# A two-stage routed feed-forward and attention kernel: scatters issued at set points, and the weight preparation in another order

## The chip, the cores and the metric

One Trainium2 chip, one of its cores. The metric is the device time of one execution in microseconds (us). A core has five engines that run their own instruction streams and meet at semaphores: PE (TensorE, matrix products and transposes into PSUM), DVE (VectorE), ACT (ScalarE), POOL (GpSimd) and SP (SyncE, here the issuer of most DMAs).

## The reference

`_layernorm` is a plain layer norm; the outer three lines are the whole computation. x is [2, 2048, 256], that is 32 tiles of 128 tokens.

```python
def ffn(h):                                  # E = 4 experts, D = 256, H = 512
    g = softmax(layer_norm(h, rn_g, rn_b) @ router_w.T)
    top2_w, top2_idx = top_k(g, 2); top2_w /= sum(top2_w) + 1e-8
    hid = relu(layer_norm(einsum('bsd,edh->bseh', h, w1), ln_g, ln_b))
    out = sum over the top 2 of top2_w * einsum('bseh,ehd->bsed', hid, w2)
    return layer_norm(out, on_g, on_b)
def attn(x):                                 # 16 heads of 16, causal, no softmax
    Q, K, V = heads(x @ Wq.T + bq), heads(x @ Wk.T + bk), heads(x @ Wv.T + bv)
    return einsum('bhtn,bhtpn->bhtp', Q, cumsum(V K^T over t)) @ Wo.T + bo
x = x + 0.5 * ffn(_layernorm(x))
x = x + attn(_layernorm(x))
x = x + 0.5 * ffn(_layernorm(x))
```

## The kernel before

The program has three stages: mixture(0), attention and mixture(1). Tokens are routed in four groups of 16 tiles. A group has two octets of 8 tiles. Within an octet each tile is normalised (`row` on ACT, `row_low` on DVE, L801), transposed (`row_T`, PE L1775 and ACT L1431) and multiplied with the router weights (`router`, PE L1792 to L1794). Then `logits`, `choose` and `place` on DVE find, for each token, its two slots in a DRAM buffer that is sorted by expert (`spos`, L855). `scatter(i)` on POOL sends tile i there with two indirect DMAs (L605). When all 16 tiles of a group are in DRAM, and the padding rows too (`pads` on SP, L452), `load_slots(p)` on SP reads slot tiles of 256 rows back: two transposing DMAs (hT, L466) and one plain one (hs, L469). Each group has 19 slot tiles, so a mixture has 38 iterations p.

An iteration of a mixture: PE computes `grams(p+2)` (L1867, L1868), `layer1(p)` (L1891 to L1893) and `layer2(p-1)` (L1906 to L1908). DVE turns the gram into a variance (`twice_low` L906, `variances` L915 and L920), POOL takes the power (`pair_std`, L613), DVE splits the result (`std_parts`, L926 and L927), and `relu_low` (L934) follows ACT's `relu_high` (L1449). SP loads slot tile p+5 and stores slot tile p-1. In the first 19 iterations of a mixture (j = 0 to 18) the next group is routed beside this; its scatters stand at j = 7 to 10 and 12 to 15, two tiles in each. Slot tile 19 is the first of the next group: SP may load it only when those scatters have landed, and SP takes its queue in order.

In attention the unit is a chunk c of 128 tokens, 32 of them. The third group is routed beside the chunks: `ROW_AT` sets the chunk from which its rows start, `LOGITS_IN` the chunks of the logits, and `MOVES` how many tiles are scattered in a chunk. Before, octet 0 is scattered in chunks 21 to 24 (two tiles each), octet 1 in chunks 29 to 31 (three, three and two).

The start of the program prepares the weights while the first group is routed. Per expert e, `centre(e)` takes the mean off the first weights (DVE L1024 to L1028, ACT L1486), `w1_T(e)` transposes them (PE L1736, ACT L1494), `w1_gram(e)` multiplies them with themselves (PE L1748, 16 fp32 products that the trace shows as one piece), and `gram_high`, `gram_low` split the result (ACT L1500, DVE L1064). `hidden_scales` finds maxima over all experts (DVE L1033), `maxima_T` and `maxima_all` bring them across the partitions (PE L1760, L1764), and `max_row`, `max_everywhere` read them (DVE L971, L976). `with_gamma` (L1054), `w1_low` (L1071), the maxima of the second weights (L1082) and `w2_low` (L1076) follow on DVE. Nothing reorders this: every engine's stream is written out by hand.

Of the kernel before, what the change touches and what calls it, by code (L numbers as in the profile page):

```python
# [5 lines left out]
ALU = mybir.AluOpType  # L6
# [3 lines left out]
F16 = mybir.dt.float16  # L10
# [4 lines left out]
P = 128  # L15
# [15 lines left out]
def macaron_kernel(nc, x, Wq, bq, Wk, bk, Wv, bv, Wo, bo, router_w, rn_g, rn_b, w1, ln_g, ln_b, w2, on_g, on_b, out):  # L31
# [30 lines left out]
    with ExitStack() as ctx:  # L62
# [24 lines left out]
        nhalf = sb("nhalf", [P, TB])  # L87
        before = sb("before", [P, E, E])
# [33 lines left out]
        h2 = at_kb(21, [2, D])  # L122
        junk = at_kb(23, [2, D], F16)
# [100 lines left out]
        def part(k, shape):  # L224
# [51 lines left out]
        (p_id, p_k, p_m, p_ws, p_c, p_mx, p_mt, p_md, p_mb, p_q, p_gam, p_w1g, p_w1h, p_w1l, p_w2h, p_w2l, p_wt, p_wtc,  # L276
         p_g, p_gh, p_gl, p_rt, p_rc, p_rw, p_on) = (sem("p_" + n) for n in (
            "identity", "constants", "m", "less_row", "centred", "maxima", "maxima_T", "maxima_diag", "maxima_all", "q",
# [98 lines left out]
        def max_bank(k):  # L377
            return bank[7] if k in (0, 3) else bank[5]
# [167 lines left out]
        def _(pool):  # L546
# [86 lines left out]
            def route(G):  # L633
# [105 lines left out]
            def attention():  # L739
# [4 lines left out]
                for c in range(NT):  # L744
# [18 lines left out]
                    for i in moves_in(c):  # L763
                        scatter(i)
# [6 lines left out]
        def _(dve):  # L771
# [214 lines left out]

            def weights():

                def scales(lo, hi):
                    step(dve.tensor_scalar(big[:, lo:hi], big[:, lo:hi], TINY, None, ALU.max))  # L990
                    step(dve.reciprocal(q[:, lo:hi], big[:, lo:hi]))
                    step(dve.tensor_tensor(q[:, lo:hi], q[:, lo:hi], capn[:, lo:hi], ALU.mult))
                    step(dve.tensor_scalar(q[:, lo:hi].bitcast(U32), q[:, lo:hi].bitcast(U32), EXPONENT, None,
                                           ALU.bitwise_and))
                    step(dve.reciprocal(qi[:, lo:hi], q[:, lo:hi]))
# [34 lines left out]
                def hidden_scales():  # L1030
# [9 lines left out]
                    all_max(1)  # L1040
# [33 lines left out]
                def w2_low(k):  # L1074
                    dve.wait_ge(p_w2h, k + 1)
                    dve.scalar_tensor_tensor(out=w2l[k][:, :, :], in0=w2r[:, :, k, :], scalar=q2, in1=w2h[k][:, :, :],  # L1076
                                             op0=ALU.mult, op1=ALU.subtract).then_inc(p_w2l, 1)

                def output_scale():
# [6 lines left out]
                    all_max(2)  # L1086
                    step(dve.tensor_copy(big[:, 3:4], mxa[:, 2, 0:1]))
                    scales(3, 4)
                    dve.tensor_scalar(kappa, sc[:, 3:4], qi[:, 3:4], None, ALU.mult).then_inc(p_q, 1)
# [24 lines left out]
                row_lows(10, 12)  # L1114
                hidden_scales()
                row_lows(12, 16)
                chain(1)
                tables(0)
                with_gamma(0)
                with_gamma(1)  # L1120
# [1054 lines left out]
```

## Time and profile before

| what | us |
|---|---|
| median of 3 executions | 1112.97 |
| lowest and highest | 1111.69, 1113.45 |
| profiled execution, device time | 1112.76 |
| its span in the trace | 1110.9 |
| preparation and first group, to the first layer1 product | 0 to 134.2 |
| mixture(0), attention, mixture(1) from there | to about 431, 762 and the end |
| PE busy over the span | 864.4 (78%) |

The page gives, for each engine, busy time and share, then 40 slices of the span, then the chain that ended last. A row of a timeline has the start in us from the start of the span, the duration in us, engine, line, operation, output and input tiles, a count, and in brackets the idle time before it and what ended that. Ends of PE rows are modelled, so a PE row can end earlier on the page than the product did.

### The profile page before, as it was taken

Reading aid. Unit: us, or ns where it says so; the run is one execution under the profiler, and the core shown is the slowest. Engines: PE = TensorE matmul, PEld = TensorE weight load, DVE = VectorE, ACT = ScalarE, POOL = GpSimd, SP = SyncE. Lnnn points to the kernel's source line nnn. Section 1 sums busy time; section 2 is a strip of 40 time slices with the busy share of each in tenths; the row PEclk is TensorE's granted clock in tenths of the full one; section 3 lists DMA queues with packets and bytes.
Section 4 is the critical chain, followed back from the end, with each engine's and each line's share of the span. In section 5 each row is a group of like instructions: output and inputs, shape, how many; then the busy total and the mean of one; then the engine's idle time right before and its main releaser. Section 6 shows DMA issues by size and latency. Waiting matters only on the chain.

```text
span 1110.9 us, 26786 instructions
## 1 busy us (share of the span) xinstructions
PE 864.4 (78%) x8660; PEld 664.8 (60%) x8660; DVE 723.6 (65%) x2096; ACT 500.8 (45%) x950; POOL 564.9 (51%) x631
## 2 busy tenths in 40 slices
PE   1534499988999797898888988974899989999600
PEld 1423278766888675556555545652787778888500
DVE  5647777576678673578778766553674775777336
ACT  2542266432444343664665655521565334444311
POOL 4046233562356451876886567463226443555373
PEclk9957599998999898998998999985999999999855
DMA  8042564674467431111112112124536567666343
GB/s 303 7 165 106 135 169 120 160 184 117 112 156 166 115 101 29 40 40 48 46 43 58 29 41 69 43 93 114 155 108 173 144 160 162 158 156 158 126 125 102
DMA packets 191146, 126.06 MB, mean 113 GB/s; under 512 B 126373, under 2 KB 180905, under 8 KB 190633
## 3 DMA queue, kind: packets, MB, share of 16 engines
q1 hardware_dynamic: 177746, 89.72, 30.7%
q0 software_dynamic: 12288, 33.57, 10.4%
q8 instruction: 79, 1.29, 0.5%
q10 hardware_dynamic: 984, 1.07, 0.3%
q14 instruction: 49, 0.40, 0.1%
HBM read 50.89 MB, written 47.19 MB: 88 GB/s over the span
## 4 chain that ended last, share of the span: by engine, by line
PE 45%; DVE 16%; issue 12%; POOL 9%; ACT 6%; DMA 5%; SPq 4%; another core or an unknown queue 3%; ACTq 0%; DVEq 0%; POOLq 0%
PE banks L1906 4%; PE banks L1891 4%; PE banks L1893 4%; PE banks L1892 4%; PE banks L1907 4%; PE banks L1908 4%; PE banks L1991 3%; SPq L518 3%; POOL slots_in L605 3%; PE banks L1993 2%; PE banks L1867 2%; PE banks L1992 2%; PE banks L1868 2%; PE banks L2106 2%
## 5 line engine op out<-in xcount | busy, mean ns | idle before, releaser
L613 POOL TENSOR_TENSOR stds<-vare,expo 128x4 f32<-128x4 f32 x76 | 80.5, 1060 | 205.7 <-DVE vare L920 205.4
L1891 PE MATMUL banks<-area,w1h 128*128 128x256 f16 x608 | 168.8, 278 | 1.0 <-DVE area L934 1.0
L1893 PE MATMUL banks<-area,w1l 128*128 128x256 f16 x608 | 168.4, 277 | 0.7 <-issue 0.7
L1892 PE MATMUL banks<-area,w1h 128*128 128x256 f16 x608 | 168.7, 277 | 0.0
L1906 PE MATMUL banks<-w2all,area 128*128 x608 | 166.2, 273 | 2.7 <-DMA w2all<-w_kept 1.9
L1908 PE MATMUL banks<-w2all,area 128*128 x608 | 165.8, 273 | 0.9 <-issue 0.8
L1907 PE MATMUL banks<-w2all,area 128*128 x608 | 165.8, 273 | 0.5 <-issue 0.5
L934 DVE SCALAR_TENSOR_TENSOR area<-banks,area 128x512 f16<-128x512 f32 x152 | 104.3, 686 | 74.6 <-ACT area L1449 59.7
L1449 ACT ACTIVATE area<-banks 128x512 f16<-128x512 f32 x152 | 89.5, 589 | 123.4 <-PE banks L1893 101.6
L605 POOL DMA_INDIRECT slots_in<-area,spos x96 | 103.5, 1079 | 78.2 <-DVE spos L855 52.5
L737 POOL TENSOR_TENSOR area<-area 128x512 f16<-128x512 f32 x64 | 81.7, 1286 | 92.9 <-ACT area L1660 92.7
L1457 ACT ACTIVATE area<-banks,stds 128x256 f32<-128x256 f32 x152 | 70.9, 466 | 90.4 <-PE banks L1908 76.0
L629 POOL DMA_INDIRECT area<-slots_out,pos x96 | 97.6, 1017 | 25.4 <-issue 22.4
L1991 PE MATMUL banks<-area 64*128 64x32 f16 (+1 forms) x766 | 75.6, 225 | 32.1 <-DVE area L1338 10.1
L1867 PE MATMUL banks<-gramh,area 128*128 x304 | 77.8, 289 | 27.5 <-issue 10.8
L915 DVE CUSTOM_DVE_ANT_0 area<-banks,area 128x256 f16<-128x256 f32 x152 | 58.3, 421 | 39.7 <-PE banks L1868 22.3
L1868 PE MATMUL banks<-graml,area 128*128 x304 | 77.8, 290 | 0.0
L1991 PEld LDWEIGHTS banks<-area 64*128 64x128 f16 (+1 forms) x766 | 39.7, 96 | 61.6 <-issue 29.3
L1993 PE MATMUL banks<-area 64*128 64x32 f16 (+1 forms) x766 | 75.0, 220 | 1.7 <-issue 1.7
L1992 PE MATMUL banks<-area 64*128 64x32 f16 (+1 forms) x766 | 74.4, 220 | 1.7 <-issue 1.7
L1660 ACT ACTIVATE area<-area 128x512 f16<-128x512 f32 x64 | 40.1, 628 | 71.5 <-DVE area L1322 65.8
L1906 PEld LDWEIGHTS banks<-w2all,area 128*128 128x128 f16 x608 | 59.3, 98 | 15.4 <-issue 3.4
(278 smaller groups left out, 2215.9 us busy)
## 6 DMA issues: line engine op xcount, KB each, us to landing
area<-slots_in SPq DMA_DIRECT2D x76, 256.0 KB
slots_out<-area SPq DMA_DIRECT2D x152, 128.0 KB
X<-in_L_attn_x_dram SPq DMA_DIRECT2D x8, 512.0 KB, 5.8
slots_in<-zrow SPq DMA_DIRECT2D x16, 256.0 KB
area<-area SPq DMA_DIRECT2D x256, 16.0 KB
out_dram<-X SPq DMA_DIRECT2D x32, 128.0 KB
area<-slots_in SPq DMA_TRANSPOSE x152
area<-in_L_ffn_w_dram SPq DMA_DIRECT2D x4, 512.0 KB, 12.5
```

What stands on the lines that cost most here:

```text
L605: pool.indirect_dma_start(slots_in[G % 2], bass.IndirectOffsetOnAxis(spos[:, O % 2, k, j:j + 1], 0), rows_of(i).rearrange("p c d -> p (c d ...
L629: pool.indirect_dma_start(d[:, i % R_C], None, slots_out[G % 2], bass.IndirectOffsetOnAxis(pos[:, G % 2, k, t:t + 1], 0)).then_inc(g_y[i % ...
L934: dve.scalar_tensor_tensor(out=Rl[:, p % 2, ms].rearrange("p m t -> p (m t)"), in0=bank[k][:, :], scalar=0.0, in1=Rh[:, p % 2, ms].rearran ...
L1867: pe.matmul(o, a[:, c], gramh[c][:, bass.ds(e, 1), :], start=(c == 0), stop=False)
L1868: last = pe.matmul(o, a[:, c], graml[c][:, bass.ds(e, 1), :], start=False, stop=(c == KC - 1))
L1891: pe.matmul(o, w1h[c][m][:, bass.ds(e, 1), :], a[:, c], start=(c == 0), stop=False)
L1892: pe.matmul(o, w1h[c][m][:, bass.ds(e, 1), :], a[:, KC + c], start=False, stop=False)
L1893: last = pe.matmul(o, w1l[c][m][:, bass.ds(e, 1), :], a[:, c], start=False, stop=(c == KC - 1))
L1906: pe.matmul(o, Rh[:, p % 2, k, rows], w2h[k][:, bass.ds(e, 1), :], start=(k == 0), stop=False)
L1907: pe.matmul(o, Rh[:, p % 2, k, rows], w2l[k][:, bass.ds(e, 1), :], start=False, stop=False)
L1908: last = pe.matmul(o, Rl[:, p % 2, k, rows], w2h[k][:, bass.ds(e, 1), :], start=False, stop=(k == HC - 1))
L1991: pe.matmul(o, lh, rh, start=start, stop=False, **kw)
```

## The change

Five things move; no arithmetic changes. One memset of 128 values (`sent`), a semaphore for it and some waits are added.

1. Scatters. In the first group, tile t of octet 0 waits until the transpose of tile t+8-1 has been copied; tiles 11 and 13 wait for the third and the fourth gram split (`p_gl`). In a mixture `pair_std(p+2)` goes ahead of both scatters, and the second waits for `relu_low(p, 0)`. In attention all but the first scatter of a chunk wait for the chunk's output product.
2. `pads(0)` on SP waits for `sent`, that is until POOL has issued all scatters of the first group.
3. Attention routes its group one chunk earlier, and scatters one tile in each of the chunks 20 to 27 and two in each of 28 to 31.
4. Preparation. On PE `w1_gram(1)` comes between the tiles 9 and 10, `w1_T(3)` between 11 and 12, `w1_gram(2)` ahead of `prefix(1)`. On DVE the rows 12 and 13 come ahead of the hidden scales, two gram splits ahead of the second octet's logits, two `with_gamma` within its chain; the second weights' maxima and the norm of X quad 4 move forward.
5. The four `w2_low` go from ahead of the first slot tile to beside the first three. The last norm's halving goes to iteration 14. `h2` and `junk` get other addresses for it.

```diff
@@ 
-        ROW_AT = 8
+        ROW_AT = 7
-        MOVES = (2, 3)
+        MOVES = (1, 2)
-            return 2 * GQ + (c - 5) // TB if c % TB == 1 and 0 <= (c - 5) // TB < GQ else None
+            return 2 * GQ + (c - 4) // TB if c % TB == 0 and 0 <= (c - 4) // TB < GQ else None
...
             def pads(G):
                 sp.wait_ge(r_pad, G + 1)
+                if G == 0:
+                    sp.wait_ge(p_sent, 1)
...
                 for t in range(GT):                      # route(), POOL
+                    if t < TO:
+                        pool.wait_ge(r_hT, t + TO)
+                    if t in (TO + 3, TO + 5):
+                        pool.wait_ge(p_gl, 3 + (t - TO - 3) // 2)
                     scatter(GT * G + t)
...
                     route(G)                             # mixture(), POOL
+                if f == 0:
+                    pool.memset(sent[:, :], 0.0).then_inc(p_sent, 1)
...
+                    if p + 2 < p0 + NP:
+                        pair_std(p + 2)
                     for t in moved[:1]:
                         scatter(GT * (G + 1) + t)
-                    if p + 2 < p0 + NP:
-                        pair_std(p + 2)
                     for t in moved[1:]:
+                        pool.wait_ge(b_Rl, 2 * p + 1)
                         scatter(GT * (G + 1) + t)
...
                     for i in moves_in(c):                # attention(), POOL
+                        if i > moves_in(c)[0]:
+                            pool.wait_ge(a_y, c + 1)
                         scatter(i)
...
                 twice_low(p0 + 1)                        # mixture(), DVE
                 std_parts(p0)
                 variances(p0 + 1)
+                if f == 0:
+                    w2_low(0)
+                    w2_low(1)
                 twice_low(p0 + 2)
                 std_parts(p0 + 1)
+                if f == 0:
+                    w2_low(2)
+                    w2_low(3)
...
                 if p == 0:                               # grams(), PE
-                    pe.wait_ge(p_q, 2)
+                    pe.wait_ge(p_gl, E)
```

DVE in the preparation, behind the row tiles 10 and 11 (L1033 are the maxima of the hidden scales, L1064 `gram_low`, L1054 `with_gamma`, `lga` the logits). Before:

```order
L801 TENSOR_TENSOR area<-h,area 128x256 x2
L1033 TENSOR_REDUCE mxw<-area 128x1 x4
...
L1048 TENSOR_SCALAR sc<-q,qi 128x1
L801 TENSOR_TENSOR area<-h,area 128x256 x4
L807 SCALAR_TENSOR_TENSOR lga<-banks,qi,r 128x32
...
L879 CAST rtab<-choice 128x19
L1054 TENSOR_TENSOR area<-area 128x1024
```

With the change:

```order
L1062 TENSOR_REDUCE mxw<-area 128x1 x4
...
L983 TENSOR_REDUCE mxr<-banks 4x1
L984 TENSOR_SCALAR mxd<-identf,mxr 4x4
L813 TENSOR_TENSOR area<-h,area 128x256 x2
L988 COPY mxa<-banks 128x4
...
L813 TENSOR_TENSOR area<-h,area 128x256 x2
L1095 SCALAR_TENSOR_TENSOR graml<-banks,sc,gramh 128x256 x4
L819 SCALAR_TENSOR_TENSOR lga<-banks,qi,r 128x32
```

Two of the four last rows stand ahead of the scales now, and two gram splits stand between the rows and the logits.

DVE at the first slot tiles (`w2all` is `w2_low`, L906 and L918 `twice_low`, `s` the parts of the standard deviation). Before:

```order
L1076 SCALAR_TENSOR_TENSOR w2all<-area,q,w2all 128x1024 x4
...
L906 SCALAR_TENSOR_TENSOR area<-area 128x512
L926 TENSOR_SCALAR s<-stds 128x2
L927 SCALAR_TENSOR_TENSOR s<-stds,s 128x2
L793 TENSOR_TENSOR r2t<-xmv,xrs 128x4
```

With the change:

```order
L932 TENSOR_SCALAR vare<-var,sc 128x2
L1015 SCALAR_TENSOR_TENSOR w2all<-area,q,w2all 128x1024 x2
L918 SCALAR_TENSOR_TENSOR area<-area 128x512
L938 TENSOR_SCALAR s<-stds 128x2
L939 SCALAR_TENSOR_TENSOR s<-stds,s 128x2
L1015 SCALAR_TENSOR_TENSOR w2all<-area,q,w2all 128x1024 x2
L805 TENSOR_TENSOR r2t<-xmv,xrs 128x4
```

The four parts no longer stand ahead of the first slot tile; the last two stand right ahead of the first iteration's row factors (`r2t`).

POOL in a mixture, octet 1 of the next group (`stds` is `pair_std`). Before:

```order
L605 DMA slots_in<-area,spos 9216x512
L613 TENSOR_TENSOR stds<-vare,expo 128x4
L605 DMA slots_in<-area,spos 9216x512 x4
L613 TENSOR_TENSOR stds<-vare,expo 128x4
...
L605 DMA slots_in<-area,spos 9216x512 x2
L613 TENSOR_TENSOR stds<-vare,expo 128x4 x4
```

With the change:

```order
L616 TENSOR_TENSOR stds<-vare,expo 128x4
L608 DMA slots_in<-area,spos 9216x512 x4
L616 TENSOR_TENSOR stds<-vare,expo 128x4
L608 DMA slots_in<-area,spos 9216x512 x4
L616 TENSOR_TENSOR stds<-vare,expo 128x4 x4
```

The 16 DMAs of an octet stood as 2, 4, 4, 4 and 2 around the powers; they stand as four times 4 now, behind a power each, with a wait in the middle of each four.

## Rows read from the trace of the kernel before

**Rows 1.** Busy time by stretch: window, us, busy (count) of each engine, PEclk, DMA, GB/s.

```profile
60.00:80.00 20.00, 4.69 (x53) 3.71 (x52) 8.49 (x26) 6.15 (x13) 10.00 (x11) 0.50 0.56 202
186.00:246.00 60.00, 56.66 (x550) 46.87 (x547) 38.67 (x146) 28.32 (x58) 36.62 (x35) 1.00 0.63 158
```

**Rows 2.** Timeline of DVE, PE and ACT, the first group's last tiles.

```profile
71.94 0.61 PE L1775 MATMUL banks<-ident,area 128*128 128x128 f16 x4 [3.92 <-issue]
75.28 0.60 ACT L1431 ACTIVATE area<-banks 128x512 f16<-128x512 f16 x1 [13.08 <-remote]
80.40 5.13 PE L1748 MATMUL banks<-area 128*128 128x256 f32 x16
```

**Rows 3.** Timeline of POOL, the first group's scatters (32 in all, 16 an octet).

```profile
87.56 0.96 POOL L605 DMA_INDIRECT slots_in<-area,spos  x1 [14.51 <-DVE spos L855]
94.71 2.12 POOL L605 DMA_INDIRECT slots_in<-area,spos  x1 [0.30 <-issue]
110.72 0.96 POOL L605 DMA_INDIRECT slots_in<-area,spos  x1 [0.30 <-issue]
```

**Rows 4.** Timeline of DVE, from the second octet's chain to the first slot tile.

```profile
94.79 1.20 DVE L1054 TENSOR_TENSOR area<-area 128x1024 f32<-128x1024 f32 x1
120.48 4.87 DVE L1076 SCALAR_TENSOR_TENSOR w2all<-area,q,w2all 128x1024 f16<-128x1024 f32 x4 [1.22 <-ACT w2all L1510]
134.32 0.16 DVE L793 TENSOR_TENSOR r2t<-xmv,xrs 128x4 f32<-128x4 f32 x1
```

**Rows 5.** Timeline of SP's queue: pads and first slot tiles; and one landing, 76 in all.

```profile
88.55 4.44 SPq L452 DMA_DIRECT2D slots_in<-zrow  x4
113.82 2.65 SPq L466 DMA_TRANSPOSE area<-slots_in  x2
124.76 0.52 SPq L469 DMA_DIRECT2D area<-slots_in  x1
768.67 0.52 SPq L469 DMA_DIRECT2D area<-slots_in  x1
772.19 0.69 DVE L906 SCALAR_TENSOR_TENSOR area<-area 128x512 f32<-128x512 f16 x1 [1.74 <-DMA area<-slots_in]
```

**Rows 6.** Timeline of PE, the start of the loop: layer1(0), then the fourth gram.

```profile
134.21 0.42 PE L1891 MATMUL banks<-area,w1h 128*128 128x256 f16 x1
141.27 0.28 PE L1867 MATMUL banks<-gramh,area 128*128 x1 [0.50 <-issue]
```

**Rows 7.** Timeline in mixture(1), the last scatters of a group and the next slots.

```profile
898.47 1.97 POOL L605 DMA_INDIRECT slots_in<-area,spos  x1 [0.30 <-issue]
902.59 2.55 SPq L466 DMA_TRANSPOSE area<-slots_in  x2
907.44 0.28 PE L1867 MATMUL banks<-gramh,area 128*128 x1 [2.88 <-DMA area<-slots_in]
```

**Rows 8.** Timeline in mixture(0): beside two, then beside four scatter DMAs in a row.

```profile
190.24 0.27 PE L1908 MATMUL banks<-w2all,area 128*128 x1
191.23 0.47 ACT L1457 ACTIVATE area<-banks,stds 128x256 f32<-128x256 f32 x1 [0.52 <-PE banks L1908]
202.53 0.27 PE L1868 MATMUL banks<-graml,area 128*128 x1
205.14 0.42 DVE L915 CUSTOM_DVE_ANT_0 area<-banks,area 128x256 f16<-128x256 f32 x1 [2.78 <-remote]
207.60 1.03 POOL L605 DMA_INDIRECT slots_in<-area,spos  x1 [0.20 <-issue]
207.98 0.68 DVE L934 SCALAR_TENSOR_TENSOR area<-banks,area 128x512 f16<-128x512 f32 x1
```

**Rows 9.** Timeline, the end of attention.

```profile
750.72 0.19 PE L1991 MATMUL banks<-area 64*128 64x32 f16 x1
755.08 0.96 POOL L605 DMA_INDIRECT slots_in<-w2all,spos  x1 [0.30 <-issue]
758.01 0.95 ACT L1670 ACTIVATE area<-banks,sc 64x256 f32<-64x256 f32 x2 [13.18 <-remote]
```

More of the change, by code:

```diff
@@ L377, in max_bank @@
         def max_bank(k):
-            return bank[7] if k in (0, 3) else bank[5]
+            return bank[7]
         def logit_bank(O):
@@ L985, in chain, with scales, output_scale, w2_low @@
                 place(O)
-            def weights():
[L989 to L995, printed above, removed]
+            def scales(lo, hi):
+                step(dve.tensor_scalar(big[:, lo:hi], big[:, lo:hi], TINY, None, ALU.max))
+                step(dve.reciprocal(q[:, lo:hi], big[:, lo:hi]))
+                step(dve.tensor_tensor(q[:, lo:hi], q[:, lo:hi], capn[:, lo:hi], ALU.mult))
+                step(dve.tensor_scalar(q[:, lo:hi].bitcast(U32), q[:, lo:hi].bitcast(U32), EXPONENT, None,
+                                       ALU.bitwise_and))
+                step(dve.reciprocal(qi[:, lo:hi], q[:, lo:hi]))
+            def output_scale():
+                max_everywhere(2)
+                step(dve.tensor_copy(big[:, 3:4], mxa[:, 2, 0:1]))
+                scales(3, 4)
+                dve.tensor_scalar(kappa, sc[:, 3:4], qi[:, 3:4], None, ALU.mult).then_inc(p_q, 1)
+            def w2_low(k):
+                dve.wait_ge(p_w2h, k + 1)
+                dve.scalar_tensor_tensor(out=w2l[k][:, :, :], in0=w2r[:, :, k, :], scalar=q2, in1=w2h[k][:, :, :],
+                                         op0=ALU.mult, op1=ALU.subtract).then_inc(p_w2l, 1)
+            def last_norm():
+                dve.wait_ge(l_on, 32)
+                dve.tensor_scalar(ong[:, :], ong[:, :], 0.5, None, ALU.mult)
+                dve.tensor_scalar(onb[:, :], onb[:, :], 0.5, None, ALU.mult).then_inc(p_on, 1)
+                dve.wait_ge(p_on, 1)
+            def weights():
                 def router_weights():
@@ L1072, in w1_low, with output_maxima @@
                                       ALU.subtract).then_inc(p_w1l, 1)
[L1074 to L1079, printed above, removed]
+                def output_maxima():
                     dve.wait_ge(l_w2, 16 * 2)
@@ L1114, in weights @@
                 row_lows(10, 12)
+                hidden_maxima()
+                max_row(1)
+                row_lows(12, 14)
                 hidden_scales()
-                row_lows(12, 16)
-                chain(1)
+                row_lows(14, 16)
+                gram_low(0)
+                gram_low(1)
+                logits(1)
+                with_gamma(0)
+                choose(1)
+                with_gamma(1)
+                place(1)
                 tables(0)
-                with_gamma(0)
-                with_gamma(1)
-                gram_low(0)
                 with_gamma(2)
-                gram_low(1)
                 with_gamma(3)
+                output_maxima()
                 gram_low(2)
+                quad_norm(GQ)
                 gram_low(3)
-                for c in range(KC):
-                    for m in range(HC):
-                        w1_low(c, m)
-                output_scale()
-                for k in range(HC):
-                    w2_low(k)
-                dve.wait_ge(l_on, 32)
-                dve.tensor_scalar(ong[:, :], ong[:, :], 0.5, None, ALU.mult)
-                dve.tensor_scalar(onb[:, :], onb[:, :], 0.5, None, ALU.mult).then_inc(p_on, 1)
-                dve.wait_ge(p_on, 1)
+                for m in range(HC):
+                    w1_low(0, m)
+                max_row(2)
+                for m in range(HC):
+                    w1_low(1, m)
             def mixture(f):
@@ L1142, in mixture @@
                     weights()
-                quad_norm(Q1)
+                    output_scale()
+                else:
+                    quad_norm(Q1)
                 twice_low(p0)
@@ L1184, in mixture @@
                         quad_norm(Q1 + j // 2 + 1)
+                    if here and f == 0 and j == OFFSET_AT:
+                        last_norm()
                     if here and OFFSET_AT <= j < OFFSET_AT + GQ:
@@ L1498, in gram_high @@
                     act.wait_ge(p_g, e + 1)
+                    if e == 0:
+                        act.wait_ge(p_q, 1)
                     for c in range(KC):
@@ L1742, in w1_gram @@
                 if e == 1:
[L1743 removed]
+                    pe.wait_ge(p_rc, 1)
                 if e >= 2:
@@ L1839, in weights @@
                 w1_T(2)
+                w1_gram(1)
                 tokens(10, 12)
+                w1_T(3)
                 maxima_T(1)
@@ L1843, in weights @@
                 tokens(12, 16)
-                w1_gram(1)
+                w1_gram(2)
                 prefix(1)
-                w1_T(3)
-                w1_gram(2)
                 w1_gram(3)
```

37 lines of the change are left out of this document (17 added, 20 removed).

## The prediction

> **What bounds the kernel now.** I read the slices of the page first: PE is busy nearly everywhere from the first layer1 product on, and hardly before it. The window rows say it in numbers [rows 1]: of the 60 us in which mixture(0) routes the next group PE is busy 56.66, DVE 38.67, POOL 36.62. Of the 20 us in the middle of the preparation PE is busy 4.69, at a granted clock of 0.50, while POOL is busy 10.00 and the DMA engines 0.56. So a mixture pays only for what stops PE or adds to it, and the preparation (134 us, an eighth of the time) is a chain through several engines, where single waits count. The change touches both.
>
> I then read the idle time in front of the preparation's rows. The transposes of two tiles at 71.94 are 0.61 long, so they should end at 72.55, yet ACT, ready for 13 us, copies them only at 75.28, and what it waited for is called "remote" [rows 2]. In that stretch POOL issues the first octet's scatters. The same shows in a mixture [rows 8]. With two scatter DMAs in a row, PE's product at 190.24 ends at 190.51 by its row and ACT reads it at 191.23. With four in a row, the gram that ends at 202.80 is read by DVE at 205.14 (2.78 idle, "remote"). Usual are 0.2 us from end to reader. So PE's products end late while POOL issues scatters: by about 0.5 beside two DMAs and 2.1 beside four, 2.7 in the preparation. At the end of attention ten stand in a row; the last small product ends by its row at 750.91, and ACT reads at 758.01 [rows 9]. The rows give no reason, only that it goes with the scatters and grows more than in proportion to how many are in a row. The change paces scatters, so this is the term on which much hangs.
>
> **Preparation, PE and the tokens.** Before, PE idles 3.92 ahead of the transposes at 71.94 [rows 2], since DVE works on the hidden scales ahead of rows 12 to 15; then comes the stall of 2.7. The fp32 Gram of the second expert starts at 80.40, when the tiles are through, and takes 5.13. With the change that Gram stands between tiles 9 and 10; in a stretch with 4.69 busy of 20 [rows 1] it lies in PE's idle time, and DVE puts two rows ahead of the scales. The tiles then end at 80.4 - 3.9 - 2.7 + 0.7 (w1_T(3), now among them, an estimate from its share of PE's time) = 74.5, plus s, what PE still runs late. In octet 0 each scatter now waits for a transposed tile seven further on, so pairs of DMAs stand apart, but they stand right where PE needs to deliver. I take s = 1.5, three times what a pair costs in rows 8; the bounds are 0 and 6 (more than both stalls of the kernel before together, 2.7 and 2.1 at four in a row).
>
> **Preparation, scatters and pads.** Octet 1's scatters start at 87.56, behind `spos`, and the last starts at 110.72 [rows 3]: 15 steps of 1.26 (0.96 and 0.30 between) are 19.0 of these 23.2 us, and 4.2 more come from stretched ones such as that of 2.12 us at 94.71. Now the Grams are out of the way of `prefix(1)`, and `spos` comes at about 85.0+s, 2.3 earlier. But tile 11 waits for gram split 3, which stands behind four `with_gamma` and the maxima on DVE, at 97.4+s by adding DVE's rows up. The last scatter ends then at 110.7+s, against 111.68. That gains little. What it costs is on SP: the pads, 4.44 us of queue at 88.55 and long landed before the scatters ended [rows 5], now wait for the last scatter. Before, `load_slots(0)` started at 113.82, 2.1 after the last scatter; now it is 110.7 + 0.2 for the memset + 4.4 + 2.1 until the pads have landed (taken as long as from the last scatter's end to SP's load) = 117.4+s: **3.6+s later**.
>
> **Preparation, DVE.** The four `w2_low`, 4.87 at 120.48 [rows 4], stood ahead of the first slot tile. This is what covers those 3.6 us: DVE would have had nothing else to do. Two of them are now done while slot tiles are on their way. The other two, 2.4 us, stand behind the third tile's `twice_low`. The third hs was issued at 124.76, and from the attention's end one takes 3.5 from issue to reader (768.67 to 772.19) [rows 5]; so it is there at 128.3 before, and 131.9+s with the change. Adding 0.6 for the splits and 2.4 gives 134.9+s for the first row factors, which stood at 134.32 [rows 4]. PE's layer1(0), at 134.21 before, needs only the first tile and its power, and comes at 131.8+s; grams(3), at 141.27 [rows 6], which hangs on the slot tile that follows, at 140.2+s. PE is the bound from there on, so the shift is between +0.6+s (factors, which PE doesn't need at once) and s-1.1 (grams(3)); nearest is what PE itself waits for. I take s-1.0 = **+0.5**; bounds -1 and +5.
>
> Beside `with_gamma` at 94.79 [rows 4] a scatter took 2.12 instead of 0.96 [rows 3]. The Trainium skill ("SBUF — State Buffer", section "SBUF: two separate sides") gives DVE and GpSimd one shared port pair that one locks out the other from; the trace agrees with its 1.2 us here. By this rule the 4.2 us of stretch go wherever DVE's large passes no longer lie beside scatters; they mostly still do, so the sum isn't changed by more than 1. The same section has it that PE waits for nobody at its ports; rows 8 show PE's readers served 2.1 late beside four scatters, so here the measurement decides, and a sum by the rule alone would give pacing no gain at all.
>
> **The mixtures.** Before, an octet's DMAs stood as 2, 4, 4, 4, 2 around the powers, now as four fours, each behind a power, with a wait for `relu_low(p, 0)` in its middle. I read whether that wait bites: the four at 207.60 begin before `relu_low` at 207.98, which ends at 208.66 [rows 8], while the third of the four would start at 210.2. It doesn't, so four stay in a row, and PE's lateness is as before: 0. That the power goes first takes at most one DMA pair from in front of it (2.5 us, POOL has slack). If the wait did bite everywhere, 4 fours in each of four octets would become pairs: 16 x (2.1 - 2 x 0.5) = 17.6 of readers' waiting; in mixture rows a third of such waits reaches PE (it is busy 94% beside them), so at best -6. Upper bound +1.
>
> The last two DMAs of a group are issued behind the fourth power rather than before it, so they end 2.5 later. In mixture(0) slot tile 19 is in SBUF by the time PE comes to it, some 5 us ahead by SP's queue: hidden. In mixture(1) it isn't: the last scatter runs at 898.47 for 1.97, SP loads at 902.59, PE starts the gram at 907.44 after waiting 2.88 for just this DMA [rows 7]. So **+2.5** (0 to +2.5).
>
> **Attention.** Octet 0 goes from four chunks with four DMAs to eight with two. By rows 8, 4 x 2.1 = 8.4 become 8 x 0.5 = 4.0; chunks are bound partly by DVE and ACT, and I take just over half of 4.4: **-2.5** (-5 to 0). Octet 1 moves from chunks of 3, 3, 2 tiles to 2, 2, 2, 2, with a wait for each chunk's output product ahead of the second tile. The last scatter started at 755.08 [rows 9]; from the scores of chunk 29 on, eight tiles of 2.53, four POOL operations of 1.15 and waits of 3.1 put its end at 755 to 756.6 against 756.04. So **0**; down to -3 if the ten in a row before 758.01 no longer delay the last chunk's products.
>
> **Sum** against the profiled execution: 1112.76 + 0.5 + 0 + 2.5 - 2.5 + 0 = **1113.3**. The profiled execution lies 0.2 under the median of 1112.97, so nothing is added. I call a change of 2.2 us (0.2%) what can be told from none.
>
> **Rivals.** A, the forecast: everything moves by small terms of both signs; 1110.8 to 1115.2 (its own range: mixture boundary 0 to +2.5, attention -4 to -1). Chance 0.37.
>
> B, slower, **the late pads and the held scatters**: s comes out at 5 rather than 1.5. The first octet's scatters wait for PE's transposes, and PE's transposes are late while scatters issue, so the two hold each other; every us of s moves `spos`, gram split 3, the last scatter, the pads and the first slot tile alike, and with `w2_low` moved away DVE has nothing to fill it with. It decides from s = 3 on. For it speaks that 75.28 shows 2.7 for one batch, and eight are now spread over the tokens; against it that PE there has idle time. 1113.3 + 3.5 to 5, about 1118. Chance 0.30.
>
> C, faster, **pacing works everywhere**: the lateness grows more than in proportion to the DMAs in a row (0.5, 2.1, 7.1 for 2, 4, 10), and the waits, even if mostly satisfied, split the fours where PE is behind (a wait for a late product holds the scatter until it is out). Mixtures -5.6, attention -3.5, its end -3, preparation -2, boundary +2.5 as before or 0: 1101 to 1107, about 1104. Against it stands 207.98. Chance 0.28.
>
> D, the change's waits are already met where they stand and only order numbers move: 1112 to 1114, within A's range. Chance 0.05, of one sign with A.
>
> **How the numbers follow.** A and D hold 0.42; of A, 0.07 falls outside 0.2% on either side together. Faster: C 0.28 and 0.05 of A's side = 0.33. Slower: B 0.30 and 0.02 = 0.32. Same: 0.35. The range takes most of B and C: 1104 to 1120.
>
> **What would show it.** In the profile after: the last first-group scatter should end near 112, `load_slots(0)` stand at 118 to 119, layer1(0) at 133, grams(3) at 141.8. Above 121 for the load means B; under 116 means C's preparation. In the mixtures, "remote" idle in front of the variances should still be 2 to 3 us beside four DMAs; if it is under 1, C is right. In mixture(1) PE should wait about 5 for the slots of the second group, and ACT's row after the last attention product should still be 5 or more late. The forecast is wrong above all if the waits bite in the mixtures, or if the preparation's token tiles end beyond 79.

## The result

The changed kernel is **slower by half a per cent**: 1116.93 us median of 20 executions (1109.25 to 1126.94) against 1111.21 us of the kernel before (20, 1105.17 to 1115.48) on the same chip; ratio 1.005, 95% interval 1.0031 to 1.0068. That is 5.6 us by the ratio, where 1113.3 against 1112.97 was forecast and up to 1120 allowed. Of the four cases the slower one, about 1118, is the nearest in time; that its mechanism was not the one at work is told below. By the prediction's own threshold of 0.2% this is "slower", which had been given 0.32, a little less than "same".

The profiled execution took 1115.16 (span 1113.4), 2.4 more than that of before. The starts of DVE's split of the standard deviation (`std_parts`, one row for each of the 76 slot tiles) cut both traces into stages that can be compared:

| stage | before | after | difference | forecast |
|---|---|---|---|---|
| start to slot tile 8 | 185.6 | 189.9 | +4.3 | +0.5 |
| mixture(0), tiles 8 to 29 | 161.7 | 161.9 | +0.2 | 0 |
| mixture(0), tiles 29 to 37 | 61.0 | 57.1 | -3.9 | 0 |
| tile 37 to 38: end of mixture(0), attention | 360.3 | 354.5 | -5.7 | -2.5 |
| mixture(1), tiles 38 to 46 | 60.3 | 62.1 | +1.8 | 0 |
| tiles 46 to 59 (scatters and group boundary) | 95.4 | 101.2 | +5.8 | +2.5 |
| tile 59 to the end | 186.8 | 186.7 | -0.1 | 0 |

The fourth stage shortened again and again in the experiments, and so did the last but one lengthen. The -3.9 of tiles 29 to 37 is one execution against another: over the other kernels this stage lies between 56.0 and 60.4 whatever their parts. So I compare stages over several profiles below, and times by their intervals.

**The preparation after.** Rows of a timeline of POOL, DVE, SP, PE and ACT of the changed kernel; they answer to [rows 3 to 6].

```profile
86.02 0.17 DVE L867 CAST spos<-sposf 128x16 uint32<-128x16 f32 x1
93.63 0.96 POOL L608 DMA_INDIRECT slots_in<-area,spos  x1 [0.30 <-issue]
98.63 0.96 POOL L608 DMA_INDIRECT slots_in<-area,spos  x1 [4.04 <-DVE graml L1095]
103.88 2.48 DVE L1102 TENSOR_TENSOR w1l<-area,w1h 128x512 f16<-128x512 f32 x4
104.06 3.14 POOL L608 DMA_INDIRECT slots_in<-area,spos  x1 [0.30 <-issue]
112.58 0.96 POOL L608 DMA_INDIRECT slots_in<-area,spos  x1 [0.30 <-issue]
114.94 3.85 SPq L455 DMA_DIRECT2D slots_in<-zrow  x4
121.37 2.66 SPq L469 DMA_TRANSPOSE area<-slots_in  x2
125.55 0.39 PE L1903 MATMUL banks<-gramh,area 128*128 x1 [20.95 <-DMA area<-slots_in]
127.09 0.69 DVE L918 SCALAR_TENSOR_TENSOR area<-area 128x512 f32<-128x512 f16 x1 [19.26 <-DMA area<-slots_in]
131.06 0.69 DVE L918 SCALAR_TENSOR_TENSOR area<-area 128x512 f32<-128x512 f16 x1 [2.19 <-DMA area<-slots_in]
136.20 2.48 DVE L1015 SCALAR_TENSOR_TENSOR w2all<-area,q,w2all 128x1024 f16<-128x1024 f32 x2
138.59 0.16 DVE L805 TENSOR_TENSOR r2t<-xmv,xrs 128x4 f32<-128x4 f32 x1
138.98 0.60 ACT L1452 ACTIVATE h<-X,xnr,xrs 128x256 f32<-128x256 f32 x1 [5.70 <-DVE xnr L806]
143.11 0.38 PE L1811 MATMUL banks<-ident,area 128*128 128x128 f16 x4 [1.08 <-ACT area L1465]
144.08 0.28 PE L1903 MATMUL banks<-gramh,area 128*128 x1 [0.58 <-issue]
```

The last scatter ends at 113.54 (111.68 before), the pads start only then, and the first slot load comes at 121.37 (113.82 before). PE stands 20.95 us and DVE 19.26 us waiting for it. The fourth gram, at 141.27 in [rows 6], is at 144.08.

**A mixture's scatters and the group boundary after**, to be held against [rows 7] and [rows 8]: timelines of POOL, DVE, SP and PE.

```profile
204.03 1.04 POOL L608 DMA_INDIRECT slots_in<-area,spos  x1 [0.20 <-issue]
205.38 0.96 POOL L608 DMA_INDIRECT slots_in<-area,spos  x1 [0.30 <-issue]
206.65 0.96 POOL L608 DMA_INDIRECT slots_in<-area,spos  x1 [0.30 <-issue]
207.92 0.96 POOL L608 DMA_INDIRECT slots_in<-area,spos  x1 [0.31 <-issue]
210.05 0.42 DVE L927 CUSTOM_DVE_ANT_0 area<-banks,area 128x256 f16<-128x256 f32 x1 [3.56 <-remote]
...
900.31 0.96 POOL L608 DMA_INDIRECT slots_in<-area,spos  x1 [0.30 <-issue]
903.42 2.55 SPq L469 DMA_TRANSPOSE area<-slots_in  x2
907.56 0.39 PE L1903 MATMUL banks<-gramh,area 128*128 x1 [4.74 <-DMA area<-slots_in]
```

The four DMAs still follow each other at 1.3 us, with the new wait in their middle, and DVE's variance behind them is no less late than before: 3.56 of "remote", against 2.78 in [rows 8]. At the boundary PE waits 4.74 for the slots instead of 2.88.

**The end of attention after**, to [rows 9]:

```profile
746.47 0.96 POOL L608 DMA_INDIRECT slots_in<-w2all,spos  x1 [0.30 <-issue]
748.74 0.95 ACT L1706 ACTIVATE area<-banks,sc 64x256 f32<-64x256 f32 x2 [7.98 <-remote]
748.98 0.96 POOL L608 DMA_INDIRECT slots_in<-w2all,spos  x1 [1.54 <-remote]
753.36 2.61 SPq L469 DMA_TRANSPOSE area<-slots_in  x2
757.42 0.39 PE L1903 MATMUL banks<-gramh,area 128*128 x1 [4.45 <-DMA area<-slots_in]
```

And two of the window rows that answer to [rows 1] (us, then busy time and count of PE, PEld, DVE, ACT, POOL, then the granted clock, the DMA share and GB/s). PE has 11.10 busy between 60 and 80 us instead of 4.69: work on the weights did move into its idle time.

```profile
60.00:80.00 20.00, 11.10 (x89) 9.04 (x88) 12.58 (x36) 12.36 (x23) 11.10 (x12) 0.66 0.61 214
186.00:246.00 60.00, 57.09 (x571) 47.12 (x569) 39.86 (x154) 27.45 (x56) 32.33 (x32) 1.00 0.56 151
```

### The profile page after: what moved, and what is told of

It is laid out like the page before. It is cut to its first block, busy times and chain, and to the rows that moved or that the text cites. A ratio compares the mean times of both kernels' runs of the same rounds, so it can differ in the third digit from the quotient of the medians.

```text
span 1113.4 us, 26788 instructions
## 1 busy us (share of the span) xinstructions
PE 859.8 (77%) x8660; PEld 657.9 (59%) x8660; DVE 723.8 (65%) x2096; ACT 502.3 (45%) x950; POOL 560.2 (50%) x632
## 3 DMA queue, kind: packets, MB, share of 16 engines
q1 hardware_dynamic: 177746, 89.72, 30.5%
q0 software_dynamic: 12288, 33.57, 10.1%
## 4 chain that ended last, share of the span: by engine, by line
PE 46%; issue 13%; DVE 13%; POOL 10%; SPq 7%; DMA 5%; ACT 4%; another core or an unknown queue 2%; ACTq 0%; DVEq 0%; POOLq 0%
POOL slots_in L608 5%; PE banks L1942 5%; PE banks L1929 4%; PE banks L1927 4%; PE banks L1944 4%; PE banks L1928 4%; PE banks L1943 4%; SPq L521 4%; PE banks L2027 3%; PE banks L1903 2%; PE banks L1904 2%; PE banks L2028 2%; PE banks L2029 2%; SPq L469 2%
## 5 line engine op out<-in xcount | busy, mean ns | idle before, releaser
L2027 PE MATMUL banks<-area 64*128 64x32 f16 (+1 forms) x766 | 74.3, 226 | 31.8 <-DVE area L1351 11.1
L2029 PE MATMUL banks<-area 64*128 64x32 f16 (+1 forms) x766 | 73.7, 220 | 1.2 <-issue 1.2
L2028 PE MATMUL banks<-area 64*128 64x32 f16 (+1 forms) x766 | 73.4, 221 | 1.0 <-issue 0.9
L918 DVE SCALAR_TENSOR_TENSOR area<-area 128x512 f32<-128x512 f16 x76 | 52.0, 684 | 32.8 <-DMA area<-slots_in 32.8
```

The costliest lines, as they stand in the source:

```text
L2027: pe.matmul(o, lh, rh, start=start, stop=False, **kw)
```

## The experiments

The three parts alone come first, then the waits and the orders in them. All ratios are to the kernel before on the same chip. Two kernels whose ratios stand 0.3% apart are not told apart by one such comparison.

### The three parts alone

`att_only` is the kernel before with the attention part:

```diff
-        ROW_AT = 8
+        ROW_AT = 7
-        MOVES = (2, 3)
+        MOVES = (1, 2)
...
                     for i in moves_in(c):
+                        if i > moves_in(c)[0]:
+                            pool.wait_ge(a_y, c + 1)
                         scatter(i)
```

(with `quad_in` as in the change). 

> The kernel before with the attention part of the change alone (rows one chunk earlier, one tile a chunk in chunks 20 to 27 and two in 28 to 31, the waits for the output product). Theory 1 (pacing pays in attention, as the profiles of before and after show between the last parts of mixture(0) and the first of mixture(1): 360.25 against 354.52 us): 5 to 6 us faster than before, about 1105.5, ratio 0.995. Theory 2 (those 5.7 us come from elsewhere, such as a slot queue that is ahead or behind): within 1.5 us of before.

Measured: ratio 0.9933 (0.9903 to 0.9963), **7 us faster**; theory 1.

`mix_only` is the kernel before with the mixture part, `pair_std` first and the wait for `b_Rl`:

```diff
+                    if p + 2 < p0 + NP:
+                        pair_std(p + 2)
                     for t in moved[:1]:
                         scatter(GT * (G + 1) + t)
-                    if p + 2 < p0 + NP:
-                        pair_std(p + 2)
                     for t in moved[1:]:
+                        pool.wait_ge(b_Rl, 2 * p + 1)
                         scatter(GT * (G + 1) + t)
```

> The kernel before with the mixture part alone (the power ahead of both scatters, the wait for relu_low(p, 0)). Theory 1 (last DMAs of an octet a whole iteration part later, so the next group's first slots come late; nothing won by the wait): 2.5 us slower in mixture(1) and 2 to 3 more in mixture(0), +3 to +6 in all. Theory 2 (only the boundary in mixture(1) pays, as predicted): +2.5. Theory 3 (pacing wins in mixtures too, hidden by something else of the change): 2 to 6 us faster.

Measured: 1.0047 (1.0019 to 1.0075), **5 us slower**. That is theory 1 by the middle value, and twice the price in the prediction; the interval alone, 2.1 to 8.4 us, still holds theory 2. `mix_nowait` below, with the same order, gives the same 5 us again. The boundary in its trace is that of the changed kernel:

```profile
916.22 0.39 PE L1868 MATMUL banks<-gramh,area 128*128 x1 [4.63 <-DMA area<-slots_in]
```

`prep_only` is the changed kernel with both of these parts as before. 

> The changed kernel with attention and mixtures as before, so the preparation part alone. Theory 1 (the later pads and first slots push everything): +4 to +5 us against before, about 1115.5. Theory 2 (the prediction's sum, later slots covered by the moved second weights): 0 to +1.5. In its trace the std parts of iteration 4 should start 4 us later than before by theory 1.

Measured: 1.0047 (1.002 to 1.0073), **5 us slower**; its tile 4 has its std parts at 158.5 against 153.8. Its first slot load is at 123.33, DVE waiting 19.10 for it. Theory 1.

The parts multiply to 0.9933 x 1.0047 x 1.0047 = 1.0027; each has an interval of about 0.003 either way, so this is not told apart from the whole, 1.005.

### The preparation: which wait

`no_sent` takes from the changed kernel the wait of the pads:

```diff
                 if G == 0:
-                    sp.wait_ge(p_sent, 1)
```

> The changed kernel without the wait of the padding rows for the last scatter. Theory 1 (this wait is what makes the first slots late): the first slot load comes 2 us after the last scatter, at 115.7 instead of 121.4; the loop begins 4 to 5 us earlier, and the kernel is 4 to 5 us faster than the changed one, about 1112.5. Theory 2 (the pads at 88 collide with the scatters of octet 1 and hold their DMAs, or the second weights' parts become the bound): less than 2 us faster.

Measured: 1.0002 (0.9973 to 1.0031), against 1.005 for the changed kernel: 5 us back, with intervals that leave 2 to 9. The timeline of its SP queue shows the pads at 88 and the load at 116.25, 2.2 behind the end of the last scatter (113.11 + 0.96):

```profile
88.06 4.52 SPq L453 DMA_DIRECT2D slots_in<-zrow  x4
116.25 2.65 SPq L467 DMA_TRANSPOSE area<-slots_in  x2
```

Tile 4 has its std parts at 152.7 instead of 158.2. The pads did not disturb the scatters beside them: octet 1's scatters end at 114.1 here and at 113.5 in the changed kernel.

`no_gl` takes only the waits for the gram splits away:

```diff
-                    if t in (TO + 3, TO + 5):
-                        pool.wait_ge(p_gl, 3 + (t - TO - 3) // 2)
```

> The changed kernel without the waits of tiles 11 and 13 for the gram splits. POOL waited 4.0 us there. Theory 1 (every us of the last scatter is one of the pads and of the loop's start): the first slot load at 117 instead of 121.4 and 3 to 4 us faster than the changed kernel, ratio to before about 1.001. Theory 2 (DVE's passes then lie beside more scatters and stretch them, so the gain is lost): ratio 1.004 to 1.006.

Measured: 1.0037 (1.0011 to 1.0063). In the trace the last scatter starts at 109.62 instead of 112.58, the load is at 118.42 instead of 121.37, and tile 4 at 153.5 instead of 158.2. So the stage gains 4.7 us in the one profile (3.0 with the load, and 1.5 that the lower clock took in the changed kernel's own profile, told further down), and the time 1.5 by the ratios, less than these can tell apart from 3 or from nothing. The time is nearest to theory 2 and the stage to theory 1, so between them it stays open.

`prep_free` is `prep_only` without either of these waits; those of octet 0's scatters for the transposed tiles stay in it. 

> The changed kernel with attention and mixtures as before and without the waits of pads and of tiles 11 and 13: the new order of the preparation without its waits. Theory 1 (order helps, waits cost): the loop's fifth iteration at 149 instead of 154, ratio 0.995 to 0.997. Theory 2 (given back): 0.998 to 1.001.

Measured: 0.9989 (0.9963 to 1.0014), in the range of theory 2. Tile 4 is at 148.5, 5.3 earlier than before: the new order, without these waits, does start the loop earlier. The time shows 1 us of that, with an interval that reaches to 4; where the rest stays is open. Its own profile ended early (span 1104.0 against 1110.9), but that is one execution on another chip.

One profile for each kernel says little, since the seven kernels with the old preparation already differ by 3.3 us at tile 4. All traces together do tell the orders apart (us, read from the timelines):

| preparation | first slot load | row factors (`r2t`) | fourth gram | tile 4 |
|---|---|---|---|---|
| old (7 traces) | 112.9 to 117.0 | 133.2 to 136.2 | 139.1 to 142.9 | 152.2 to 155.5 |
| new, both waits (after, prep_only) | 121.4, 123.3 | 138.6, 140.5 | 144.1, 146.0 | 158.2, 158.5 |
| new, gram waits only (no_sent) | 116.3 | 133.4 | 138.8 | 152.7 |
| new, pads' wait only (no_gl) | 118.4 | 135.6 | 141.0 | 153.5 |
| new, neither (prep_free, best2, best3) | 111.8 to 112.4 | 129.0 to 129.5 | 134.4 to 134.9 | 148.3 to 149.1 |

In the seven traces of the new order the factors follow the first load by 17.1 to 17.2 and the fourth gram follows it by 22.5 to 22.7, whenever the load comes. In the old order the gram follows the load by 25.8 to 27.5. So the new order makes the stretch behind the load 3 to 5 us shorter, and its two waits make the load 9 to 12 us later than the same order without them.

### Attention: spreading or waiting

`att_nowait` is `att_only` without the two lines of the wait. 

> The kernel before with the attention part, but without the wait for the output product. The attention part in full gave ratio 0.993. Theory 1 (spreading pays: one tile a chunk for eight chunks; the wait adds nothing in octet 0, where a chunk has one tile, and is met in octet 1): 0.993 again, and attention 352 us. Theory 2 (what pays is the wait at the end, which keeps the last chunk's products from running behind ten scatters): about 0.998, and ACT again reads the last product some 7 us after its row ends.

Measured: 0.9911 (0.9881 to 0.9941). The same kernel was run again later as `spread_again`. 

> The spread attention without waits on the kernel before, once more, so that it stands on the same chip as the two above. Its ratio was 0.991, interval 0.988 to 0.994. Expected the same by every theory; were it over 0.995, the comparison of chips would not bear differences of 0.3%.

Measured: 0.9972 (0.9943 to 1.0). The two intervals just miss each other, for one and the same kernel; with `att_only` the mean of three is 0.994. (The ratios are not the quotients of the medians, and these differ less here: 1102.17 / 1110.23 = 0.9927 and 1103.35 / 1109.25 = 0.9947.) The expectation made 0.995 the point from which comparisons across chips can't bear 0.3%: so they can't, and I don't say from the times whether the wait helps. The traces do, since the last four chunks repeat themselves there: to 0.1 us with the scatters as before, to 1.4 at most in the other groups. DVE's `update_x`, one for each chunk, gives (us):

| | chunk 19 to 27 | 27 to 31 | update of 31 to the std parts of tile 38 |
|---|---|---|---|
| scatters as before (before, mix_only, mix_nowait, mix_split, prep_only, prep_free) | 76.5 to 78.8 | 38.1 to 38.2 | 6.2 to 6.3 |
| spread, with wait (after, att_only, no_sent, no_gl, best2) | 76.7 to 80.3 | 30.5 to 31.9 | 10.2 to 10.4 |
| spread, no wait (att_nowait, spread_again, best3) | 75.5 to 80.7 | 33.2 to 33.5 | 6.4 |

Spreading octet 0 (chunks 20 to 27) gave nothing. Spreading octet 1 shortened the last four chunks by 4.7, and the wait took another 2.5 off them (means of the groups). But the wait also puts the last scatter later against the chunk, and PE then waits for the slots, so that the wait costs 4.0 behind it: in all it loses 1.4. The rows of `att_nowait`, where eight DMAs stand in a row up to 747.27, show ACT reading late as in [rows 9], after a wait of 10.66 instead of 13.18, and no wait for a DMA after it:

```profile
746.31 0.96 POOL L605 DMA_INDIRECT slots_in<-w2all,spos  x1 [0.30 <-issue]
748.79 0.95 ACT L1670 ACTIVATE area<-banks,sc 64x256 f32<-64x256 f32 x2 [10.66 <-remote]
749.42 2.61 SPq L466 DMA_TRANSPOSE area<-slots_in  x2
755.06 0.39 PE L1867 MATMUL banks<-gramh,area 128*128 x1 [2.04 <-issue]
```

One thing in attention was not looked for: chunks 8 to 19, in which nothing is scattered, take 107.7 to 112.8 in the eight traces with the attention part and 113.6 to 117.4 in the six without. The means differ by 4.2 us. Part of that is only moved: the quads are normalised one chunk earlier, and the chunk before, 7 to 8, takes 10.1 instead of 8.1 to 8.8. From chunk 0 to 19, which holds all of it, the means differ by 3.2 us (183.9 to 190.6 against 188.5 to 195.4, so the ranges overlap). The third group's rows and quads being one chunk earlier was not run alone, so it is the likely cause of these 3 us and not a shown one.

### The mixtures: order, wait, and a row that is really split

`mix_nowait` is `mix_only` without the wait. 

> The kernel before with the power ahead of both scatters and no wait between them. The full mixture part gave 1.005. Theory 1 (the wait is always met, the order is what costs): 1.005 again, fours in rows as with the wait. Theory 2 (the wait holds scatters back and makes the group late): 1.001 or less.

Measured: 1.0052 (1.0026 to 1.0077), as with the wait. The order costs; the wait is met wherever POOL comes to it, since its rows are broken at the same place (0.81 us, once in mixture(1)) with the wait and without.

`mix_split` puts the wait where it bites:

```diff
-                        pool.wait_ge(b_Rl, 2 * p + 1)
+                        pool.wait_ge(b_Rl, 2 * p + 2)
```

> As the mixture part alone, but the second scatter waits for relu_low(p, 1), half an iteration later, so that rows of four DMAs do become rows of two. Theory 1 (lateness grows more than in proportion to the row, so pairs are cheaper): 5 us faster than the mixture part alone, ratio to before about 1.000, and no idle of over 1.5 us called remote in front of the variances. Theory 2 (lateness is paid per DMA): no faster than the mixture part alone, 1.005.

Measured: 1.0004 (0.9977 to 1.003), 5 us faster than `mix_nowait` on the same chip. POOL's timeline shows the wait biting, where PE and DVE have got behind it:

```profile
214.91 1.04 POOL L605 DMA_INDIRECT slots_in<-area,spos  x1 [0.20 <-issue]
216.25 0.96 POOL L605 DMA_INDIRECT slots_in<-area,spos  x1 [0.30 <-issue]
219.72 1.16 POOL L605 DMA_INDIRECT slots_in<-area,spos  x1 [2.51 <-DVE area L935]
221.19 0.96 POOL L605 DMA_INDIRECT slots_in<-area,spos  x1 [0.30 <-issue]
```

It does so in some rows only: the four before, at 208.74 to 212.65, are still unbroken, and idle called "remote" ahead of the variances is still there (7.6 us in three places in mixture(1), DVE's waits between 825 and 905), against what theory 1 wanted. That sum is a poor witness, though: over the same stretch it is 6.2 in the kernel before and 0 in `mix_only`, which differs from `mix_split` by the wait alone. So the time speaks for theory 1 and the waits say nothing; that pairs are cheaper than fours is not shown.

Over all profiles, mixture(1)'s tiles 46 to 59 (us):

| order | tiles 46 to 54 | tiles 54 to 59 |
|---|---|---|
| old (before, att_only, att_nowait, prep_only, best2, best3, prep_free, spread_again) | 60.8 to 62.7 | 33.6 to 36.5 |
| new (after, mix_only, mix_nowait, no_sent, no_gl) | 60.3 to 64.8 | 36.6 to 38.7 |
| new, split | 60.0 | 38.0 |

So 3.0 of the order's 5 lie at the boundary (means 34.8 and 37.8); the split gives nothing back there. The remaining 2 would fit the scatters before it, tiles 46 to 54 (means 61.3 and 62.5), or mixture(0), tiles 8 to 29 (means 162.1 and 164.3), but single profiles of one order differ by up to 4 and 7 there, so their place stays open. Where the split gains its 5 us stays open too.

### What is left when the costs are taken out

`best2` is the changed kernel with mixtures in the old order and neither of the preparation's waits. 

> The changed kernel without its two costs as the parts showed them: mixtures in the order of before, pads not waiting for the scatters, tiles 11 and 13 not waiting for gram splits. Theory 1 (the parts add: attention -7, preparation 0 or less): ratio 0.991 to 0.994, faster than both kernels. Theory 2 (what one part gives another takes): above 0.997. If the waits for the gram splits cost their 4 us on POOL, the last scatter of the first group ends at 108 instead of 113.5.

Measured: 0.9948 (0.9924 to 0.9971), 1104.72 us beside 1110.23. That is faster than both kernels, and between the theories: the parts as measured (0.9933 x 0.9989 = 0.992) are inside the interval. The last scatter ends at 109.75 and not at 108, the load is at 111.94, and the loop's tile 4 at 148.3.

`best3` also drops the wait in attention. 

> The changed kernel with mixtures in the order of before, without the waits of pads, of tiles 11 and 13 and of the scatters in attention: the free preparation and the spread attention together. Theory 1 (the loop starts 5 us earlier with the free preparation and keeps that): 0.991 - 0.004 = 0.987. Theory 2 (the start's gain is given back before the end, as the version with the attention waits, 0.995, already let one think): 0.991 to 0.994, no better than spread attention alone.

Measured: 0.9932 (0.9901 to 0.9962), 1102.14 us beside 1109.25, **faster than both kernels**: 7 us under the one before, about 13 under the changed one by the ratios. On its chip it stood 4 us under spread attention alone by the ratios (0.9972), but 1.2 by the medians, and the intervals overlap: that the free preparation adds to spread attention is not shown. 0.987, which counts the whole of the earlier start, is outside its interval; as with `prep_free`, not all of what the earlier start gives reaches the end.

## Why the prediction was right in its numbers, and where its steps weren't

The time lay in the range, and the sign was left open (0.33, 0.35, 0.32). The sum of +0.5 came out as +5.6 by the ratio and as +2.4 between the two profiles. Three terms were each too small, two of them up and one down: about +4 in the preparation, +2 in the mixtures, -4 in attention. That the errors cancelled in part was luck, and the range of 16 us was wide against a change of 5.6.

**Preparation, +0.5 forecast, +4.3 by the stages, +5 by the part alone: the term that failed.** s, how late PE runs, was put at 1.5. `spos` should have come at 85.0+s and is written at 86.2, so s was 1.2; by the tiles, forecast to end at 74.5+s and over at 74.3, it was nothing. That step held. With it falls the rival B in the form it was given, scatters and products that hold each other up, although the load came at 121.37, beyond the 121 that the prediction had named as B's sign. The hold of tile 11 was forecast for 97.4+s and lasted until 98.63: right.

Behind it the load was sized 2.5 us too early. The last scatter ended at 113.5 instead of 112.2, because one scatter took 3.14 beside `w1_low` (103.88 for 2.48), and the sum of stretched scatters had been left unchanged. And from the last scatter to the load 7.8 us passed where 6.7 were summed (1.4 to the first pad, 3.9 for four, 2.6 until landed): 121.37 instead of 118.9.

The second step that failed is the choice of what PE waits for. From the load to the row factors the sum was 17.5 (134.9 less 117.4), and all seven traces have 17.1 to 17.2. So the factors were +0.6+s, that is +2.1, even by the prediction. It took s-1.0 all the same, because PE "doesn't need [them] at once". It does: ACT waits 5.70 us for them and makes the token rows at 138.98, PE transposes these up to 143.11, and the fourth gram stands behind the transposes in PE's stream. In the seven traces of the new order the gram follows the factors by 5.4 to 5.5. Ahead of the factors stands the second pair of `w2_low` (136.20 for 2.48).

The cover by `w2_low` was right as far as it was claimed: the load came 7.6 us later and the first `twice_low` no later (127.09 against 127.72), the fourth gram 2.8 later. But DVE was idle for 19.26 us ahead of the first slot tile, with all four `w2_low` behind it, two of them on the path. What the kernel gains if they go back into that gap was not run. `no_sent` shows that the late load is the cause: with the pads early, the load is 5.1 us earlier, the fourth gram 5.2 and tile 4 5.5.

The granted clock made up the rest in this one profile: the fourth gram is 2.8 us later than before, the fifth 4.3. PE was idle 1.69, 1.08 and 0.58 us between 140 and 144, and its layer1 rows at 145.10 to 147.45 run at 0.42 us each and not 0.27.

```profile
146.00:150.00 4.00, 4.00 (x38) 2.88 (x37) 3.29 (x12) 1.09 (x2) 1.11 (x1) 0.72 0.88 186
```

The clock granted in this window was 0.72 of full speed (a mix of 1.2 and 2.4 GHz), where it was 1.00 in the kernel before. Twelve products at 0.21 us apart instead of 0.11 are 1.2 us of the 1.5. In `prep_only` the clock stayed up there; its load was 2 us later still, and its tile 4 came out as late.

**Mixture(1)'s boundary, +2.5: right, at 3.0.** PE's wait grew from 2.88 to 4.74 (4.63 in the part alone, 4.25 without the wait).

**The mixtures' rest, 0: right on the wait, short on the size.** That the wait would be met was the reading of [rows 8], and the unbroken fours and `mix_nowait` bear it out. What the new order costs beside the boundary, about 2 us by the ratios and their intervals, had been given an upper bound of +1. Rival C, that pacing works everywhere, was wrong for these waits; `mix_split` has one that bites and is 5 us faster than the same order without it.

**Attention, -2.5 for octet 0 and 0 for octet 1: the sum's sign right, both places wrong.** The profile gave -5.7, the part alone -7. Octet 0's chunks did not change beyond what single profiles differ by, so the price of late products taken over from [rows 8] is not paid there; why was not tested. Octet 1 gave -7.3 in the last four chunks and took back 4.2 in the wait for the slots, in all -3.1, at the edge of its bound of -3 and not at its value of 0. About 3 us came from the chunks before the scatters, which the prediction didn't consider.

**The shared port.** In the changed kernel one scatter takes 3.14 us beside `w1_low`, where 0.96 is usual, and in the six other kernels with the new preparation one takes 2.54. The Trainium skill ("SBUF — State Buffer", section "SBUF: two separate sides") has it that a DVE pass with two inputs in SBUF and a GpSimd instruction that reads SBUF take turns at one port pair. The 2.2 us extra beside 2.48 us of passes agree with that. The other four passes of `w1_low` do not: at 100.97 they lie beside scatters as well and stretch them by 0.4 us in all, and before, all eight (4.95 us at 106.50) stretched theirs by 1.0. So the length of a pass is no measure here of what it costs a scatter.

## What to carry to other kernels

When a wait delays the first transfer of a queue, follow the delay to every consumer and take the one that comes last on the path; don't drop one because it isn't needed "at once". Here the row factors looked harmless, and in seven traces the loop's start hung on them at a fixed distance from the first load. Look for an engine's idle time ahead of the late transfer and ask what of the moved work could stand there. A wait for pacing changes nothing where it is always met; where it bites, the last transfer of the group is later too, so spread the group over more steps before you add the wait.

## What the runs showed that was not expected

Products of PE are read late while POOL issues scatters, but the lateness doesn't follow the length of the row, as the prediction had it (0.5, 2.1, 7.1 for 2, 4, 10). Its 7.1 was read from a row that isn't the last product; this one is:

```profile
751.43 0.17 PE L1993 MATMUL banks<-area 64*128 64x32 f16 x1 [0.50 <-issue]
```

It ends at 751.60, 6.4 us ahead of the reader. At the same place the traces have 5.7 to 7.0 us behind ten scatters in a row, 7.0 behind eight and 2.9 to 4.3 behind six. What they share is the end of the row: in all fourteen traces ACT begins 1.3 to 2.0 us after the last scatter of the row has ended (758.01 after 756.04 before, 748.74 after 747.43 with the change, 748.79 after 747.27 in `att_nowait`). Of all 176 waits of ACT and DVE over 2 us that these traces call "remote", 109 end 0.8 to 2.1 us behind a row too, though 47 end inside one. So at the end of attention a late product costs what is left of the row when it is done, and about 1.5 us more, and the shorter last row is the likely source of the 4.7 us that the last four chunks gain. Why the readers wait for the row's end, no trace here shows.

The executions of one kernel spread over 8 to 18 us, and the longer ones tend to have the lower mean granted clock (0.913 in one of 1109.25 us of the changed kernel, 0.898 in one of 1122.16). Two measurements of one kernel, `att_nowait` and `spread_again`, came out 0.6% apart by their ratios. Stages and distances that repeat to 0.1 or 0.2 us in many traces told apart what the times could not.
